# A ViT tower layer on one core: patches of a third image, weight splits, semaphores of biases and running sums, and the order of routing and table steps moved

## Chip, cores, metric

The kernel runs on one core of one Trainium2 chip. The metric is the device time of one execution in microseconds (us). Before the change it was 1286.59 us, the median of three executions (1285.31 to 1288.26).

## What is computed

The reference takes 16 images of 5 x 128 x 128 and computes one tower layer in float32:

- patch embedding: 256 patches of 320 values per image, times W, then a layer norm with gamma;
- attention on the layer-normed tokens, 16 heads of 64: q and k through silu, decay weights exp(cum_i - cum_j) from a running sum of -softplus(x Wa + ba), `attn = (q k) * decay` below the diagonal, `o = attn v`, a norm over each head, a sigmoid gate, the output product, added to the tokens;
- a mixture of experts on the layer-normed result: router logits, softmax, the best 2 of 8 experts, `gelu(x w1 + b1) w2 + b2` of each, weighted and added.

## The kernel before

Each engine has a hand-written stream of instructions, and semaphores tie the streams. The order of the work is the order of the calls in each stream; nothing plans it.

**Start.** SyncE (SP) loads the patches of images 0 and 1, waits for the embedding weight and for image 1's patches, issues the loads of attention weights 0 and 1, then the patches of image 2 (into `xt`, image 0's buffer, so only once image 0 is embedded), then weights 2 and 3. TensorE (PE) runs `tokens(0)`, `tokens(1)`, `turn(0)` (transposes), `tokens(2)`, `turn(1)`, `logits(0)`, the first `queries`, `cum(0)` and so on. Between `tokens` and `turn` lie VectorE's (DVE) `embed` and `embed_norm` and a power on GpSimd (POOL). ScalarE (ACT) and DVE split each weight into a rounded high part (`weight_hi`, line 803) and the rest (`weight_lo`, line 1697); products with split operands take three matmuls. `store_cum` writes the running sums to DRAM in six transfers that count on one semaphore, and `load_decay` reads them back, spread over the partitions, into a ring of four slots (`dec_x`).

**Attention.** Images go in pairs, p = 0 to 7. Step (p, c) with c = 0 to 7 handles two heads of pair p; the same step carries the embedding of pair p + 1, and normalisation, output product and routing of pairs before. `last_step` is c = 7. ACT forms the decays (`decay`, line 838), DVE multiplies them onto the scores (`decayed`, line 1720), PE then runs `weighted` (line 1243). Routing of an image is `turn2` (line 1282, transposes), ACT `keep_x2`, PE `route` (line 1290), DVE `keep_logits` and `choose`, then `ranks`. After 5 pairs (EARLY) `first_tables` (lines 1886 to 1901), 15 small steps on DVE that each wait for the one before, computes from the counts which expert and which rows the first blocks take. It stands in step (7, 0) and waits for a table loaded by `first_constants`.

**Experts.** Rows of tokens were scattered by expert into lists in DRAM. Blocks 0 to 3 (256 rows, plain float32, `early1` line 1339 and `early2` line 1352, one call per chunk c of 8 of the hidden width) are interleaved by hand with the end of attention. Then come whole blocks with split operands (`layer1` line 1538, `layer2` line 1550), and at the end 9 mixed rows: a whole block followed by a unit of 128 rows (`one1` line 1563, `one2` line 1574). Per block, SP loads weights, second-layer bias (`load_b2`, line 414), rows (line 417, or 423 for a unit) and first-layer bias (`load_b1`, line 411). SP also writes padding to the lists (line 597), four transfers in each of two blocks. Both biases of a block count on one semaphore `b_in`, for which ACT waits before the first gelu (line 908) of a block. DVE's `keep_y` (line 1971) adds the second bias, `row_tails` (lines 1957 to 1964) reads token number and router weight from the rows, and `hidden_lo` (line 1987) makes the low part of the hidden values. POOL scales the result (line 716) and adds it to the output by an indirect transfer (line 722), whose landing counts on `added`. SP may refill the row buffer only once `row_tails` has read it.

In `mixed_row`, the stream of DVE before the change is:

```python
for c in range(HC):
    hidden_lo(k, c)
    if c >= HC - WQ and not last:
        w_lo("w1", w1_sp[1 - b_par], w1_stage[1 - b_par], k.b + 1, c - (HC - WQ))
    if c == 2:
        keep_y(before, pieces)
    if c == 4:
        row_tails(k, rows_f[0], BS)
```

## Time and profile before

| | before |
|---|---|
| median of three executions | 1286.59 us |
| profiled execution | 1284.18 us |
| its span, first to last instruction | 1282.3 us |
| PE busy | 1243.4 us (97%), 8534 matmuls |
| ACT, DVE, POOL busy | 858.1, 824.9, 426.6 us |
| mean granted clock of PE | 0.993 of full |

The span runs from the first to the last instruction; 1.9 us of the execution lie around it. A share near 100% names the engine to look at, and the stretches in which that engine stands idle are what other work holds it up for. The granted clock is 1.0 at 2.4 GHz and 0.5 at 1.2 GHz. Times within the span are counted from its start.

### The profile page before, as it was taken

The page shows a single profiled execution, that of the slowest core. Times are in us where ns is not written, and L with a number is a line of the kernel's source. Part 1 is how long each engine was busy: PE and PEld are TensorE (multiplying, and loading weights), DVE is VectorE, ACT ScalarE, POOL GpSimd, SP SyncE. Part 2 cuts the span into 40 slices and gives each one's busy share as a digit, 9 for nine tenths or more (in the row PEclk, how much of TensorE's full clock was granted, in tenths as well). Part 3 has the DMA queues.
Part 4 walks back from the last instruction along what each step waited for, and adds up shares of the span by engine and source line. Part 5 has one row for each costly group of instructions (what it writes and reads, how often), then busy time and mean ns, then how long its engine had stood idle before and what let it go on. Part 6 is the DMA issues. An engine that isn't in the chain of part 4 may idle for free. (4 is left out here: it accounts for less than half of the span.)

```text
span 1282.3 us, 27300 instructions
## 1 busy us (share of the span) xinstructions
PE 1243.4 (97%) x8534; PEld 1068.5 (83%) x8534; DVE 824.9 (64%) x2120; ACT 858.1 (67%) x2019; POOL 426.6 (33%) x524
## 2 busy tenths in 40 slices
PE   6999999999999999999999999999999999999996
PEld 5777788788787877877877777889999999999995
DVE  5455565666666667666566566557788888565561
ACT  4767666667658557567567566447788888666672
POOL 2211121242151241141241151354354454433433
PEclk8999999999999999999999999999999999999998
DMA  5532222233233233232232237288988887989883
GB/s 189 168 101 84 92 88 91 85 113 107 81 115 109 78 117 109 69 126 92 78 123 68 94 118 241 91 239 248 259 230 246 220 225 190 276 264 269 253 238 82
DMA packets 125607, 194.46 MB, mean 152 GB/s; under 512 B 16272, under 2 KB 91504, under 8 KB 125360
## 3 DMA queue, kind: packets, MB, share of 16 engines
q1 hardware_dynamic: 110864, 175.37, 43.1%
q0 software_dynamic: 13584, 17.26, 6.6%
q8 instruction: 54, 0.88, 0.3%
q10 hardware_dynamic: 1056, 0.55, 0.2%
q14 instruction: 49, 0.40, 0.1%
HBM read 167.40 MB, written 29.05 MB: 153 GB/s over the span
## 5 line engine op out<-in xcount | busy, mean ns | idle before, releaser
L1193 PE MATMUL bank<-xn_sp,big_r 128*128 128x512 f32 x1152 | 312.0, 408 | 1.0 <-DVE xn_sp L1692 1.0
L1193 PEld LDWEIGHTS bank<-xn_sp,big_r 128*128 128x128 f32 x1152 | 204.4, 188 | 54.2 <-issue 1.7
L1720 DVE TENSOR_TENSOR att<-bank,dec_x 128x384 f32<-128x384 f32 x256 | 130.5, 551 | 100.6 <-PE bank L1232 95.2
L838 ACT ACTIVATE dec_x<-dec_x,ncum 128x256 f32<-128x256 f32 (+1 forms) x512 | 189.8, 445 | 6.7 <-POOL dec_x L665 6.7
L665 POOL TENSOR_SCALAR_AFFINE_SELECT dec_x<-dec_x 128x256 f32<-128x256 f32 x256 | 108.1, 450 | 226.7 <-DMA dec_x<-cum_scratch 226.2
L1538 PE MATMUL bank<-big_r 128*128 128x256 f32 x1296 | 169.1, 287 | 2.2 <-ACT mid_f L908 2.2
L1538 PEld LDWEIGHTS bank<-big_r 128*128 128x128 f32 x1296 | 162.0, 193 | 3.3 <-ACT mid_f L908 2.4
L716 POOL TENSOR_SCALAR mid_f<-mid_f,dec_x 128x256 f32<-128x256 f32 x71 | 76.3, 1080 | 185.1 <-DVE mid_f L1971 180.0
L1987 DVE TENSOR_TENSOR big_r<-mid_f,big_r 128x256 fp32r<-128x256 f32 x216 | 91.3, 423 | 70.8 <-ACT big_r L928 70.8
L722 POOL DMA_INDIRECT out<-mid_f,tok x71 | 118.8, 1673 | 51.9 <-POOL mid_f L716 21.0
L908 ACT ACTIVATE mid_f<-bank,h 128x256 f32<-128x256 f32 x216 | 101.3, 478 | 42.3 <-PE bank L1538 20.2
L808 ACT ACTIVATE tq<-bank 128x512 f32<-128x512 f32 x64 | 38.3, 598 | 112.9 <-PE bank L1193 112.8
L1978 DVE TENSOR_TENSOR big_r<-big_f,big_r 128x512 fp32r<-128x512 f32 x148 | 101.7, 691 | 8.1 <-ACT big_r L902 1.0
L1186 PE MATMUL bank<-big_r,xn_sp 128*128 128x512 f32 x384 | 98.8, 397 | 0.0
L1271 PEld LDWEIGHTS bank<-big_r,y_sp 128*128 128x128 f32 x768 | 95.5, 191 | 1.9
L1271 PE MATMUL bank<-big_r,y_sp 128*128 128x256 f32 x768 | 96.8, 284 | 0.0
L813 ACT ACTIVATE tq<-bank 128x512 f32<-128x512 f32 x64 | 38.1, 596 | 86.5 <-PE bank L1193 86.4
L902 ACT ACTIVATE big_r<-big_f 128x512 fp32r<-128x512 f32 x148 | 93.6, 637 | 0.0
L928 ACT ACTIVATE big_r<-mid_f 128x256 fp32r<-128x256 f32 x216 | 91.7, 425 | 0.0
L1243 PE MATMUL bank<-att,mid_f 128*64 128x256 f32 x512 | 85.0, 404 | 6.4 <-DVE att L1720 5.0
L687 POOL DMA_INDIRECT expert_rows<-xn,slot x64 | 65.4, 1022 | 76.2 <-DVE slot L1855 60.1
L1229 PE MATMUL bank<-q_s,k_s 64*128 64x256 f32 x512 | 89.9, 428 | 0.3 <-DVE k_s L1711 0.3
(230 smaller groups left out, 2216.2 us busy)
## 6 DMA issues: line engine op xcount, KB each, us to landing
big_f<-in_L_ffn_w SPq DMA_DIRECT2D x68, 1024.0 KB, 7.9
dec_x<-cum_scratch SPq DMA_DIRECT2D x128, 384.0 KB, 3.7
big_w<-in_L_ffn_w SPq DMA_DIRECT2D x12, 1024.0 KB, 6.2
mid_f<-expert_rows SPq DMA_DIRECT2D x27, 261.0 KB, 3.2
h_scratch<-h SPq DMA_DIRECT2D x16, 256.0 KB, 2.3
h<-h_scratch SPq DMA_DIRECT2D x8, 512.0 KB, 4.2
out<-h SPq DMA_DIRECT2D x16, 256.0 KB, 4.1
xt<-in_x SPq DMA_DIRECT2D x15, 256.0 KB, 3.9
```

Source lines behind the costliest of these rows:

```text
L665: pool.affine_select(out=d, in_=d, pattern=[[0, 2], [1, P]], compare_op=ALU.is_ge, fill=fill, base=0, channel_multiplier=-1).then_inc(M["c ...
L722: pool.indirect_dma_start(out=out_rows, out_offset=bass.IndirectOffsetOnAxis(ap=tok[k.par][:, s:s + 1], axis=0), in_=yo[k.par][:, s, :], i ...
L838: act.activation(d, d, ACT.Exp, bias=ncum[p % 2][:, NS * u + s, 2 * c + hh:2 * c + hh + 1]).then_inc(M["exp_done"], 1)
L902: act.activation(parts[0].rearrange("p k n -> p (k n)")[:, cols], staged[:, cols], ACT.Copy).then_inc(M[f"{name}_hi"], 1)
L908: act.activation(target, bank[hbank[c % HB]][:, 0:width], ACT.Gelu_apprx_tanh, bias=b1_sb[k.par][:, c:c + 1]).then_inc(M["gel_done"], 1)
L928: act.activation(g_sp[0][:, c, :], gel[c % NGEL], ACT.Copy).then_inc(M["gh_done"], 1)
L1186: mm = pe.matmul(bank[target][:, :], xp[:, k, t * P:(t + 1) * P], wp[:, k, n * 512:(n + 1) * 512], start=(k == 0 and j == 0), stop=(k == E ...
L1193: mm = pe.matmul(bank[target][:, :], wp[:, k, c * P:(c + 1) * P], xp[:, k, :], start=(k == 0 and j == 0), stop=(k == EC - 1 and j == 2))
L1271: mm = pe.matmul(bank[target][:, s * E:(s + 1) * E], yp[:, j, u * S + s * P:u * S + (s + 1) * P], wp[:, GC * g + j, :], start=(j == 0 and ...
L1538: mm = pe.matmul(bank[hbank[c % HB]][:, 0:BLK], wp[:, i, c * P:(c + 1) * P], xp[:, i, :], start=(i == 0 and j == 0), stop=(i == EC - 1 and ...
L1720: dve.tensor_tensor(att[hh][:, :], bank[4 + hh][:, 0:LW], dec[n % RING][:, hh, :], ALU.mult).then_inc(M["mult_done"], 1)
L1978: dve.tensor_tensor(lo, staged[:, cols], f32(hi), ALU.subtract).then_inc(M[f"{name}_lo"], 1)
```

## The change

- The patches of image 2 get a buffer of their own, slot 3 of the decay ring, and are loaded right after those of image 1; each of the first three images has a semaphore. SP issues the attention weights once the embedding weight and image 0's patches are in.
- PE runs 5 matmuls on zeros before its first wait (`keep_running`), and 5 more between `tokens(1)` and `turn(0)`. A memset of `att0` on DVE feeds them.
- ACT splits weights 1, 2 and 3 later in its stream, behind `keep_xnT(0)`, `xn_hi(0)` and `keep_cum(0)`.
- The running sums of each image of a pair count on a semaphore of their own. So do first-layer and second-layer biases: ACT waits for the first only, `keep_y` for the second.
- `route(11)` moves from step (6, 6) to the last step of pair 6. Around the end of attention, `early1`, `early2`, `gn_mean`, `turn2` and `route` are reordered on PE, and `keep_x2` and the gelus on ACT to fit.
- In the last step of pair 7, DVE runs `decayed(7, 7, 1)` ahead of `head_stats` and `y_lo`.
- `first_tables` moves from step (7, 0) to (7, 2); in its place one copy keeps the counts (`cnt1`).
- In mixed rows `row_tails` follows `keep_y` at c = 2 instead of standing at c = 4.

New semaphore names are left out.

```diff
...
-        side_x = [xt, mid_f[:, 2048:2048 + (KT + 1) * S].rearrange("p (k n) -> p k n", k=KT + 1)]
+        side_x = [xt] + [x.rearrange("p (k n) -> p k n", k=KT + 1) for x in
+                         (mid_f[:, 2048:2048 + (KT + 1) * S], dec_x[:, 3 * 2 * LW:4 * 2 * LW])]
...
+        def patches(n):
+            return side_x[n if n < 3 else 0]
...
         tr1 = room(232, N1)
+        cnt1 = room(242, X)
...
             def load_patches(n):
-                have(sp, "tok_ps", {1: 0, 2: 1}.get(n, n))
-                image, to, m = xT[:, n * S:(n + 1) * S], of(n, side_x), "xt_in1" if n == 1 else "xt_in"
+                have(sp, "tok_ps", n if n > 2 else 0)
+                image, to, m = xT[:, n * S:(n + 1) * S], patches(n), f"xt_in{n}" if n < 3 else "xt_in"
...
                         t = NS * u + s
-                        sp.dma_start(cum_d[p, u, :, cols:cols + P], cumT[t * H:(t + 1) * H, :]).then_inc(M["cum_out"], 16)
+                        sp.dma_start(cum_d[p, u, :, cols:cols + P], cumT[t * H:(t + 1) * H, :]).then_inc(M[f"cum_out{u}"], 16)
...
                 have(sp, "mult_done", 2 * (n - RING + 1))
-                sp.wait_ge(M["cum_out"], 96 * (p + 1))
+                sp.wait_ge(M[f"cum_out{u}"], 48 * (p + 1))
...
             def load_b1(e, par):
-                sp.dma_start(b1_sb[par], b1[bass.ds(e, 1), :, :].rearrange("a p k -> (a p) k")).then_inc(M[f"b_in{par}"], 16)
+                sp.dma_start(b1_sb[par], b1[bass.ds(e, 1), :, :].rearrange("a p k -> (a p) k")).then_inc(M[f"b1_in{par}"], 16)
...
             def load_b2(e, par):
-                sp.dma_start(b2_sb[par], b2[bass.ds(e, 1), :].broadcast_to([P, E])).then_inc(M[f"b_in{par}"], 16)
+                sp.dma_start(b2_sb[par], b2[bass.ds(e, 1), :].broadcast_to([P, E])).then_inc(M[f"b2_in{par}"], 16)
...
             load_patches(1)
+            load_patches(2)
...
             sp.wait_ge(M["wt_in"], 32)
-            sp.wait_ge(M["xt_in1"], 32)
+            sp.wait_ge(M["xt_in0"], 32)
...
             load_weight(1)
-            load_patches(2)
...
                 act.wait_ge(M["ct_ps"], p + 1)
-                have(act, "cum_out", 96 * p)
+                have(act, "cum_out0", 48 * p)
+                have(act, "cum_out1", 48 * p)
...
                 if c == 0:
-                    act.wait_ge(M[f"b_in{k.par}"], 32 * (k.n + 1))
+                    act.wait_ge(M[f"b1_in{k.par}"], 16 * (k.n + 1))
...
             weight_hi(0)
+            keep_xnT(0)
...
             weight_hi(1)
-            keep_xnT(0)
-            weight_hi(2)
...
             xn_hi(0)
-            weight_hi(3)
+            weight_hi(2)
...
             keep_cum(0)
+            weight_hi(3)
...
             keep_x2(2 * NPR - 2)
-            active_early(1, 4)
+            for c in range(4, HC):
+                active_early(1, c)
...
             keep_x2(2 * NPR - 1)
-            for c in range(5, HC):
-                active_early(1, c)
...
         def _(pe):
+            def keep_running(n):
...
+                for i in range(n):
+                    pe.matmul(bank[5][:, 0:E], att[0][:, 0:P], att[0][:, P:P + E], start=True, stop=True)
...
+            pe.wait_ge(M["cleared"], 1)
+            keep_running(5)
...
             pe.wait_ge(M["wt_in"], 32)
-            pe.wait_ge(M["zeroed"], 3)
+            pe.wait_ge(M["zeroed"], 4)
...
             def tokens(n):
-                if n == 1:
-                    pe.wait_ge(M["xt_in1"], 32)
+                if n < 3:
+                    pe.wait_ge(M[f"xt_in{n}"], 32)
...
                 else:
-                    pe.wait_ge(M["xt_in"], 32 * max(n, 1))
+                    pe.wait_ge(M["xt_in"], 32 * (n - 2))
...
                     for k in range(KT + 1):
-                        mm = pe.matmul(bank[embed_bank(n)][:, s * E:(s + 1) * E], of(n, side_x)[:, k, s * P:(s + 1) * P], wt[:, k, :],
+                        mm = pe.matmul(bank[embed_bank(n)][:, s * E:(s + 1) * E], patches(n)[:, k, s * P:(s + 1) * P], wt[:, k, :],
...
                     tokens(2 * p + 4)
+                elif pair(p - 1):
+                    route(2 * p - 1)
...
                     turn2(2 * p - 2, "s1_z", min(p + 2, NPR), 6)
-                if c == 6 and post:
+                if c == 6 and post and p != NPR - 2:
...
             pe.wait_ge(M["c_sum"], 32)
+            keep_running(5)
...
             early1(0, 2)
+            early1(0, 3)
...
             gn_mean(NPR - 1, 1, "lg_done", 2 * NPR - 2)
-            early1(0, 3)
...
             out_proj(NPR - 1, 1, 1, 7, "h2_done", 2 * NPR - 1)
-            early2(0, 4)
-            early2(0, 5)
+            for c in range(4, HC):
+                early2(0, c)
...
             turn2(2 * NPR - 2, "h2_done", 2 * NPR)
-            early2(0, 6)
-            early2(0, 7)
+            early1(1, 4)
+            early1(1, 5)
...
             route(2 * NPR - 2)
-            early1(1, 4)
-            turn2(2 * NPR - 1, "lg_done", 2 * NPR - 1)
-            early1(1, 5)
-            route(2 * NPR - 1)
...
             early1(1, 7)
+            turn2(2 * NPR - 1, "lg_done", 2 * NPR - 1)
...
             early2(1, 0)
+            route(2 * NPR - 1)
...
-            def first_tables():
...
-                dve.wait_ge(M["tb1_in"], 16)
+            def first_counts():
...
                 dve.wait_ge(M["h_out"], 16 * B)
+                dve.tensor_copy(cnt1, cnt).then_inc(M["cnt1_done"], 1)
...
+            def first_tables():
...
+                dve.wait_ge(M["tb1_in"], 16)
+                dve.wait_ge(M["cnt1_done"], 1)
...
                 cmp1 = cut1.rearrange("p (a n) -> p a n", a=N1)
-                t1(dve.tensor_tensor(cut, cnt.rearrange("p (n a) -> p n a", a=1).broadcast_to([P, X, N1]), iob1, ALU.is_ge))
+                t1(dve.tensor_tensor(cut, cnt1.rearrange("p (n a) -> p n a", a=1).broadcast_to([P, X, N1]), iob1, ALU.is_ge))
...
                 dve.wait_ge(M["y_ps"], k.j + 1)
+                dve.wait_ge(M[f"b2_in{k.par}"], 16 * (k.n + 1))
...
                 if main:
+                    if p == NPR - 1:
+                        decayed(p, 7, 1)
...
                     y_lo(p, 0, 0)
-                    decayed(p, 7, 1)
+                    if p < NPR - 1:
+                        decayed(p, 7, 1)
...
                     if p == NPR - 1:
-                        first_tables()
+                        first_counts()
...
                         embed(2 * p + 3)
+                    if p == NPR - 1:
+                        first_tables()
...
+            dve.memset(att[0][:, :], 0.0).then_inc(M["cleared"], 1)
...
                         keep_y(before, pieces)
-                    if c == 4:
...
             def earlier(k):
-                return k._replace(j=k.j - 1, par=1 - k.par, r1=k.r1 - 2)
+                return k._replace(j=k.j - 1, par=1 - k.par, n=k.n - 1, r1=k.r1 - 2)
```

## Rows read from the trace of the kernel before

**Rows 1.** The page, section 1: busy time, share of the span, instructions

```profile
PE 1243.4 (97%) x8534; PEld 1068.5 (83%) x8534; DVE 824.9 (64%) x2120; ACT 858.1 (67%) x2019; POOL 426.6 (33%) x524
```

**Rows 2.** Waits of PE, whole span: total us, times, longest us

```profile
PE bank L1143 <- DMA wt<-in_L_tok_W: 6.2, 1, 6.2
PE bank L1243 <- DVE att L1720: 5.0, 5, 1.7
PE bank L1310 <- DMA mid_f<-expert_rows: 4.3, 5, 1.5
PE bank L1538 <- ACT mid_f L908: 2.2, 1, 2.2
```

**Rows 3.** Windows: length, then busy us (count) PE, PEld, DVE, ACT, POOL; clock, DMA share, GB/s

```profile
25.50:32.30 6.80, 6.42 (x19) 4.56 (x18) 5.45 (x7) 4.31 (x7) 0.00 (x0) 0.50 0.01 2
902.70:906.10 3.40, 3.40 (x18) 3.40 (x18) 2.99 (x6) 3.40 (x10) 0.00 (x0) 0.50 0.88 316
```

**Rows 4.** Timeline of the start, PE and DVE: start us, us, instruction [idle before <-releaser]

```profile
6.23 5.49 PE L1143 MATMUL bank<-wt,xt 128*128 128x256 f32 x12 [6.23 <-DMA wt<-in_L_tok_W]
...
11.51 2.92 PE L1143 MATMUL bank<-wt,mid_f 128*128 128x256 f32 x12
...
11.83 0.70 DVE L1641 BATCH_NORM_STATS2 st<-bank 128x6 f32<-128x512 f32 x1 [10.06 <-PE bank L1143]
```

**Rows 5.** DMA issues of ACT's queue at the start: KB, us to landing (issued at 3.69)

```profile
wa_sb<-in_L_attn_Wa ACTq DMA_DIRECT2D x1, 16.0 KB, 5.4
```

**Rows 6.** Timeline, pair 6 to 7, ACT and the PE instruction that waits

```profile
698.50 0.58 ACT L843 ACTIVATE big_f<-bank 128x512 f32<-128x512 f32 x1
...
699.13 0.65 PE L1243 MATMUL bank<-att,mid_f 128*64 128x256 f32 x4 [1.31 <-ACT big_f L843]
```

**Rows 7.** Timeline, step (7, 0): first and last step of the tables, and PE

```profile
728.03 0.24 DVE L1886 TENSOR_TENSOR h<-taken,xt 128x80 f32<-128x80 f32 x1 [2.76 <-DMA xt<-in_c_first]
...
731.50 0.17 DVE L1901 TENSOR_TENSOR h<-h 128x8 f32<-128x8 f32 x1
...
732.78 0.81 PE L1243 MATMUL bank<-att,mid_f 128*64 128x256 f32 x3 [1.69 <-DVE att L1720]
```

**Rows 8.** Timeline of DVE, end of step (7, 2)

```profile
747.54 1.22 DVE L1762 SCALAR_TENSOR_TENSOR big_f<-big_f 128x1024 f32<-128x1024 f32 x1
750.18 1.02 DVE L1720 TENSOR_TENSOR att<-bank,dec_x 128x384 f32<-128x384 f32 x2 [1.42 <-PE bank L1232]
```

**Rows 9.** Timeline of PE in the same stretch, and at the end of step (7, 7)

```profile
752.96 0.65 PE L1243 MATMUL bank<-att,mid_f 128*64 128x256 f32 x4
...
796.19 0.80 PE L1243 MATMUL bank<-att,mid_f 128*64 128x256 f32 x3 [0.74 <-DVE att L1720]
```

**Rows 10.** Timeline of PE, routing of the last pair

```profile
823.90 1.89 PE L1352 MATMUL bank<-big_w,k_s 128*128 128x256 f32 x8
826.73 0.63 PE L1282 MATMUL bank<-ident,xn 128*128 128x128 f32 x4 [0.94 <-DVE xn L1794]
...
832.04 0.66 PE L1282 MATMUL bank<-ident,xn 128*128 128x128 f32 x4 [1.20 <-DVE lg L1799]
```

**Rows 11.** Timeline, a whole block's first gelu, the rows of PE ahead of and behind it

```profile
896.97 3.04 PE L1550 MATMUL bank<-y_sp,big_r 128*128 128x256 f32 x24
901.65 0.84 ACT L908 ACTIVATE mid_f<-bank,h 128x256 f32<-128x256 f32 x2 [5.32 <-DMA h<-in_L_ffn_b]
```

**Rows 12.** DMA issues from 890.5 to 891.0: KB, us to landing

```profile
big_f<-in_L_ffn_w SPq DMA_DIRECT2D x2, 1024.0 KB, 10.6
```

**Rows 13.** Timeline, first mixed row: DVE, POOL, PE, SP

```profile
1095.50 0.69 DVE L1971 TENSOR_TENSOR mid_f<-bank,tq 128x512 f32<-128x512 f32 x1 [0.36 <-PE bank L1550]
...
1098.32 3.12 PE L1550 MATMUL bank<-big_r 128*128 128x256 f32 x24
...
1100.15 1.60 POOL L722 DMA_INDIRECT out<-mid_f,tok  x1 [1.84 <-DMA out<-mid_f,tok]
...
1102.01 0.37 SPq L417 DMA_DIRECT2D mid_f<-expert_rows  x1
```

More of the change, by code:

```diff
@@ L291, in vit_layer @@
         names = """
-        passed mh_done zeroed c_in c_sum ws_in0 ws_in1 ws_in2 ws_in3 ws_hi ws_lo wt_in g_in
-        xt_in xt_in1 tok_ps s1_st s1_u s1_v0 s1_v1 s1_st2 s1_ve s1_rs s1_h s1_xn
+        cleared passed mh_done zeroed c_in c_sum ws_in0 ws_in1 ws_in2 ws_in3 ws_hi ws_lo wt_in g_in
+        xt_in0 xt_in1 xt_in2 xt_in tok_ps s1_st s1_u s1_v0 s1_v1 s1_st2 s1_ve s1_rs s1_h s1_xn
         s1_tps s1_xnT s1_aps s1_z h_out sp_abs sp_e sp_l sp_m sp_la gnh
-        xh_done xl_done cum_ps cc_done ncum_done ct_ps ct_copied cum_out
+        xh_done xl_done cum_ps cc_done ncum_done ct_ps ct_copied cum_out0 cum_out1
         dec_in0 dec_in1 dec_in2 dec_in3 causal exp_done
@@ L300, in vit_layer @@
         tope_done trec_done wall_done idxf_done pick_done both_done rk_ps rank_done taken_done rsel_done
-        slot_done tail_done scat0 scat1 scat2 scat3 late_out tb1_in tb_in wf_in0 wf_in1 wf_in2 wf_in3 w1_inx tb1
+        slot_done tail_done scat0 scat1 scat2 scat3 late_out tb1_in cnt1_done tb_in wf_in0 wf_in1 wf_in2 wf_in3 w1_inx tb1
         tb pad_out
-        row_in0 row_in1 w1_in0 w1_in1 w2_in0 w2_in1 b_in0 b_in1 xe_ps xe_hi xe_lo w1_hi w1_lo w2_hi w2_lo
+        row_in0 row_in1 w1_in0 w1_in1 w2_in0 w2_in1 b1_in0 b1_in1 b2_in0 b2_in1 xe_ps xe_hi xe_lo w1_hi w1_lo w2_hi w2_lo
         hid_ps gel_done gh_done gl_done y_half y_ps y_done ecol_done wk_done wsel_done y_w added
@@ L1877, in along @@
                 return x.rearrange("p (a n) -> p a n", a=1).broadcast_to([P, n, X])
+            def first_counts():
+                dve.wait_ge(M["taken_done"], EARLY)
+                dve.wait_ge(M["h_out"], 16 * B)
+                dve.tensor_copy(cnt1, cnt).then_inc(M["cnt1_done"], 1)
             def first_tables():
                 dve.wait_ge(M["tb1_in"], 16)
-                dve.wait_ge(M["taken_done"], EARLY)
-                dve.wait_ge(M["h_out"], 16 * B)
+                dve.wait_ge(M["cnt1_done"], 1)
                 cut = cut1.rearrange("p (n a) -> p n a", a=N1)
                 cmp1 = cut1.rearrange("p (a n) -> p a n", a=N1)
-                t1(dve.tensor_tensor(cut, cnt.rearrange("p (n a) -> p n a", a=1).broadcast_to([P, X, N1]), iob1, ALU.is_ge))
+                t1(dve.tensor_tensor(cut, cnt1.rearrange("p (n a) -> p n a", a=1).broadcast_to([P, X, N1]), iob1, ALU.is_ge))
                 t1(dve.tensor_reduce(nb1, cut, AX.X, ALU.add))
```

## The prediction, made before the changed kernel was run

> **What bounds the kernel.** I read the page's busy shares first. PE is busy for 1243.4 us of a span of 1282.3 [rows 1], so everything hangs on PE: its work, its clock, and the 39 us in which it stands idle. The other engines have a third of their time free. The change adds no useful matmul and removes none, so the gain can only come out of idle time and of stretches at the lower clock. The waits of PE [rows 2] are therefore the second view: they tell how much each kind of releaser costs. A busy ScalarE or VectorE elsewhere costs nothing. The third view is the granted clock in windows: 25.5 to 32.3 and 902.7 to 906.1 ran at 0.50, which is 1.2 GHz [rows 3]. PE was idle for 2.17 us just before the second of them [rows 2]. The first 12 matmul records took 5.49 us, the next 12 of the same shape 2.92 us [rows 4], so the start was at the lower level too, although it is not marked as such. Only then do I go to the timeline around each edit. The sum below is made against the profiled execution (1284.18 us, 1282.3 of it span); the median, 1286.59, lies 2.4 us above it, and I subtract the same gain from both.
>
> **1. The start.** Five matmuls on zeros begin after one memset, near 1.3 us. At the cold duration (two records of 5.49 / 12 = 0.46 us each) they take 4.6 us and end near 5.9, before the weight lands at 6.23, so they delay nothing. If they raise the clock, `tokens(0)` takes 2.9 us instead of 5.5 and ends 2.6 us earlier, near 9.1. `embed(0)` follows at 11.83 now [rows 4]. It also waits for the constants on ACT's queue, the last of which was issued at 3.69 and took 5.4 us, so 9.1 [rows 5]. Now image 2's patches (320 KB) and the first attention weights are in flight beside them. I allow 0.5 us for that: `embed(0)` starts near 9.7, 2.1 us earlier than before. Behind it lies a serial chain (DVE, POOL, DVE, PE, twice), then the high parts on ACT, all of which move along; the second five matmuls fill a gap that is otherwise idle. The low parts of the weights were never the last to come while their order on DVE is unchanged, and weights now load about 2 us earlier, so the chain keeps its lead down to the first scores. **2.1 us**, between 0 (clock not raised) and 2.6. The stretch at 0.50 from 25.5 held 6.42 us of busy PE [rows 3], so its removal would give another 3.2; the idle gaps and light matmuls ahead of it stay, so I count nothing and keep 3.2 for the range. Splitting the running sums' semaphore gives nothing: the decays that it releases sooner next queue on ACT behind the same evacuations. If that cover went, it would be worth half a microsecond.
>
> What ACT's queue suffers from a full SP queue is not shown directly. The Trainium skill (DMA: Bandwidth & Descriptors, Queues, rings and completion order) says that every DMA engine takes turns, packet by packet, between the queues that have work, which speaks against loading a third image so early. By that rule the constants share the engines with up to 320 KB more; at some 300 GB/s that would be an estimated 1.1 us instead of my 0.5, and the sum would be 0.6 us smaller.
>
> **2. `route(11)` moved.** PE waits 1.31 us at 699.13 for ACT's copy of 698.50 [rows 6]. The moved matmuls fill that wait and leave the step before shorter. But ACT's copy stands behind a run of ACT work that does not wait for PE, so PE arrives earlier and still starts at 699.13. **0**, between 0 and 1.3. The logits come a little later on DVE; they are read early in the next step, far from the end.
>
> **3. `first_tables`.** In step (7, 0) DVE stands for 2.76 us on a table's load, then works from 728.03 to 731.67, and PE waits 1.69 us for the product behind it [rows 7]. In step (7, 2) the table has landed. DVE is free from 747.54 + 1.22 = 748.8, 3.6 us of tables end at 752.4, and the next product, at 750.18 now [rows 8], starts then. PE wants it at 752.96 [rows 9] and gets its first half some 0.6 us after the start: 0.1 to 0.2 us late. The copy of the counts is one short instruction. The experts' first loads wait for the tables two steps later than before, but stand in step (7, 4) anyway. **1.5 us**, between 1.0 and 1.7.
>
> **4. `decayed(7, 7, 1)` first.** It releases the 0.74 us at 796.19 [rows 9]; `head_stats` and `y_lo` move behind it, and their reader, `gn_mean`, gets one more `early1` ahead of it as cover. **0.7 us**, between 0.3 and 0.7.
>
> **5. Routing of the last pair.** PE waits 0.94 us for the normed rows and 1.20 us for logits [rows 10]. A chunk of `early2` takes 1.89 / 2 = 0.94 us. Four of them from 823.90 on last to 827.6, past 826.73, so the first wait goes. Three more chunks of `early1` stand ahead of the second `turn2`, which is reached near 832.3, past 832.04. Late next are the ranks, since the last `route` now comes after `turn_early(2)` and one chunk while only two chunks cover DVE's choice of experts: 0.25 us. **1.9 us**, between 0.8 and 2.1.
>
> **6. Biases.** At 901.65 ACT had waited 5.32 us for a second-layer bias that the gelu does not read [rows 11]. PE ran dry at 900.0 and lost 2.17 us [rows 2], and then had 3.4 us at half clock [rows 3], worth 1.7. With its own semaphore the gelu starts as soon as ACT is free, near 896.3. `keep_y` waits for the bias instead, most of a row later, when it has landed; `hidden_lo` is queued behind it. What could be late next is the following block's weights: two loads just ahead of that bias took up to 10.6 us [rows 12]. If the first of them landed only then, near 900.8, ACT would stop in its third operation and PE would still lose about 1 us. I take **3.9 us**, since 1 MB ahead of 2 MB should land well before the median of both, between 0.5 and 3.9.
>
> **7. Row tails.** In mixed rows PE waits 5 times for rows of the next whole block, 4.3 us in all, at most 1.5 [rows 2]. SP issues that load right behind the row tails, at 1102.01 in the first mixed row [rows 13]. `keep_y` there starts at 1095.50. Moved behind it, the row tails come up to 3 us earlier, and SP's issue with them. Against it stands a new wait: row tails need the earlier adds to have landed, shown by POOL at 1100.15 [rows 13]. So in this row DVE holds `hidden_lo(3)` until 1100.15 + 1.0 for the tails + 0.4 = 1101.5. PE's second layer, from 1098.32 in four chunks of 0.75, wants it at 1100.6: 0.9 to 1 us lost, and 0.5 of the 1.5 gained here. In the other rows I expect the adds in time. 4.3 - 1.0 = **3.3 us**, between -2 and 4.3.
>
> **Sum.** 2.1 + 0 + 1.5 + 0.7 + 1.9 + 3.9 + 3.3 = 13.4 us. The profiled execution would take 1270.8 us, the median 1286.6 - 13.4 = 1273.2. A measurement of this kernel can tell about 0.2%, or 2.6 us, from no change.
>
> **Rivals.**
> - *The cold stretch at 25.5 goes too.* The work ahead of it shifts by 2 us and has ten more matmuls. For: PE's activity before it changes. Against: the light matmuls and gaps just before 25.5 remain. 13.4 + 3.2 gives 1270.0. Chance 0.17.
> - *Gaps are handed on.* The clock is not raised in time, so that the start gives nothing, and the weights replace the bias at 896 (0.5 instead of 3.9). For: the transfers of [rows 12]. 13.4 - 2.1 - 3.4 = 7.9 gives 1278.7. Chance 0.17.
> - *Slower, through the row tails.* DVE, in nine mixed rows, holds `hidden_lo(3)` behind a landing. PE wants it 5.1 us after `keep_y` starts, and tails and low part take 1.4 of it, so that adds may land 3.7 us after that start; in [rows 13] they land 4.65 after. Each later microsecond costs nine. Without term 7 the gain is 10.1; with a loss of 1.4 us in each row (landings at 5.1 in all nine) it becomes a loss of 2.5, the point from which this decides; at 5.7 it is 18 - 10.1, or 1294.5. Against: PE's waits of today would then shrink too, and `keep_y` waits for almost the same adds already. Chance 0.05.
> - *Nothing to measure.* Every gap comes back behind the next releaser: within 2.6 us of 1286.6. Chance 0.03.
>
> The forecast itself keeps 0.58. The range goes from the first rival with all of term 7 (1269.0, and 1.0 for the scatter of the runs: 1268.0) to the second with term 7 halved (1278.7 + 1.7, about 1280.5). Faster by over 0.2%: 0.58 + 0.17 + 0.17 = 0.92; same 0.03; slower 0.05.
>
> **What would show it.** Term 1: the first `tokens` matmuls near 0.24 us a record, `embed(0)` before 10, the first scores some 2 us earlier. Term 2: PE's wait at the last step of pair 6 longer than 1.31 or ending at the same relative time. Term 3: no wait of DVE for the table, PE's wait in step (7, 1) gone. Terms 4 and 5: those PE waits gone, one of 0.25 before the ranks. Term 6: ACT's wait for a bias absent, clock 1.00 near 900. Term 7: PE's waits for rows at most one. The forecast is wrong if PE idles over 30 us in the new trace, or if new waits of PE for `hidden_lo` fill the mixed rows.

## The result, and the profile after

| | before | after |
|---|---|---|
| median of seven executions | 1286.59 us | 1279.52 us (1274.47 to 1282.02) |
| profiled execution, its span | 1284.18, 1282.3 us | 1277.72, 1275.6 us |
| PE busy | 1243.4 us | 1247.3 us |

The ratio is 0.9933, 95% interval 0.9913 to 0.9953. The ratio goes by all executions and not by the medians: by the medians the changed kernel is 7.1 us faster, by the ratio 8.6, with an interval of 6.0 to 11.2. That is inside the predicted range, but little more than half of the 13.4 us I forecast. (In one of the kernels below, the start undone, one of eight executions took 3056.25 us and counts in no ratio.) The profiled executions differ by as much (6.5 us), so their two traces can be laid side by side, term by term. The page's first line after, which answers to [rows 1]:

```profile
PE 1247.3 (98%) x8554; PEld 1071.8 (84%) x8554; DVE 828.7 (65%) x2123; ACT 857.0 (67%) x2019; POOL 429.5 (34%) x524
```

And of the waits of PE five lines, which answer to [rows 2] (total us, times, longest us):

```profile
PE bank L1322 <- DMA mid_f<-expert_rows: 4.8, 6, 1.7
PE bank L1255 <- DVE att L1733: 2.8, 4, 1.6
PE bank L1155 <- DMA wt<-in_L_tok_W: 1.7, 1, 1.7
PE bank L1563 <- DVE big_r L2006: 0.6, 1, 0.6
PE bank L1311 <- DVE both L1839: 0.4, 1, 0.4
```

The wait for the gelu (2.2 in [rows 2]) and the two for routing [rows 10] are gone, and the waits for attention fell from 5.0 to 2.8. The waits for expert rows, which term 7 was to remove, grew from 4.3 to 4.8 and are now the first line (L1322, before L1310), and a new one for the low part of the hidden values stands behind (L2006). PE's busy time rose by 4 us with twenty records more, those of the matmuls on zeros, which are busy for 6.8 us: busy is not useful here.

**The start.** Timeline of PE and DVE, after (line 1155 was 1143, 1654 was 1641, 1241 was 1229):

```profile
7.43 2.86 PE L1155 MATMUL bank<-wt,xt 128*128 128x256 f32 x12 [1.70 <-DMA wt<-in_L_tok_W]
...
10.88 0.70 DVE L1654 BATCH_NORM_STATS2 st<-bank 128x6 f32<-128x512 f32 x1 [8.31 <-DMA wa_sb<-in_L_attn_Wa]
...
38.92 0.70 PE L1241 MATMUL bank<-q_s,k_s 64*128 64x256 f32 x4 [0.25 <-DVE k_s L1724]
```

The window at the low clock, columns as in [rows 3], and the constant's issue, columns as in [rows 5]:

```profile
22.34:32.60 10.26, 10.13 (x32) 7.89 (x32) 7.22 (x9) 7.66 (x11) 0.00 (x0) 0.51 0.01 2
```

```profile
wa_sb<-in_L_attn_Wa ACTq DMA_DIRECT2D x1, 16.0 KB, 7.2
```

The zeros did what they were to do: the first twelve token matmuls take 2.86 us instead of the 5.49 of [rows 4]. But `embed(0)` waits for the last constant now, which takes 7.2 us instead of the 5.4 of [rows 5], and starts at 10.88 rather than 9.7. And the stretch at 0.50, 6.8 us in [rows 3], lasts 10.3. PE's first scores start at 38.92; before it was 39.02.

**Tables, `decayed` and routing.** PE, after (line 1255 was 1243):

```profile
699.04 0.65 PE L1255 MATMUL bank<-att,mid_f 128*64 128x256 f32 x4 [1.11 <-ACT big_f L849]
...
750.95 0.80 PE L1255 MATMUL bank<-att,mid_f 128*64 128x256 f32 x3 [0.22 <-DVE att L1733]
...
834.75 0.38 PE L1311 MATMUL bank<-both,strict 128*128 128x32 f32 x2 [0.38 <-DVE both L1839]
```

The wait of 1.31 [rows 6] is 1.11 at the same place, and it ends 660.1 us behind the first scores in both kernels, so that moving `route(11)` gave nothing. The 1.69 of [rows 7] is 0.22 two steps later, which makes 1.47. The 0.74 of [rows 9] is gone. Of the 2.14 of [rows 10] there is 0.38 left, before the ranks, where I had put 0.25.

**Biases.** Window 890 to 910, after, same columns:

```profile
890.00:910.00 20.00, 20.00 (x169) 19.91 (x168) 17.22 (x40) 17.54 (x45) 8.51 (x6) 1.00 1.03 307
```

PE is busy throughout at full clock: the 2.17 us and the half-clock stretch of [rows 3, 11] are gone.

**Mixed rows.** Timeline of the first two, after: SP, then DVE, then PE (SP lines 412, 419, 422 load second-layer weights, second-layer bias and rows; DVE 1975 is the first instruction of `row_tails`):

```profile
1089.49 3.42 SPq L419 DMA_DIRECT2D tq<-in_L_ffn_b  x1
1094.28 0.37 SPq L422 DMA_DIRECT2D mid_f<-expert_rows  x1
...
1109.20 1.52 SPq L412 DMA_DIRECT2D big_f<-in_L_ffn_w  x2
1113.41 0.37 SPq L422 DMA_DIRECT2D mid_f<-expert_rows  x1
...
1091.71 0.15 DVE L1975 COPY dec_x<-h 128x1 f32<-128x1 f32 x1 [3.92 <-DMA out<-mid_f,tok]
...
1092.91 0.98 PE L1563 MATMUL bank<-big_r 128*128 128x256 f32 x6 [0.61 <-DVE big_r L2006]
...
1100.29 0.66 PE L1322 MATMUL bank<-ident,mid_f 128*128 128x128 f32 x4 [1.74 <-DMA mid_f<-expert_rows]
...
1120.71 0.66 PE L1322 MATMUL bank<-ident,mid_f 128*128 128x128 f32 x4 [1.03 <-DMA mid_f<-expert_rows]
```

DVE now stands 3.92 us for an add before it can make the low parts, and PE is held up by that. The rows' load in the second row is issued 4.2 us after the pair of weight loads (1109.20 to 1113.41), where before it was 6.2 (SP, then the PE instruction that waits):

```profile
1116.47 1.52 SPq L407 DMA_DIRECT2D big_f<-in_L_ffn_w  x2
...
1122.70 0.37 SPq L417 DMA_DIRECT2D mid_f<-expert_rows  x1
...
1127.67 0.66 PE L1310 MATMUL bank<-ident,mid_f 128*128 128x128 f32 x4 [0.72 <-DMA mid_f<-expert_rows]
```

How long these two loads took, after and before:

```profile
mid_f<-expert_rows SPq DMA_DIRECT2D x1, 261.0 KB, 7.3
mid_f<-expert_rows SPq DMA_DIRECT2D x1, 261.0 KB, 4.9
```

PE, which waits for the landing in both kernels, starts on the rows 11.5 us after the weights' issue now (1120.71) and 11.2 us after it before (1127.67). Over the eight such loads of the mixed rows the issue stands on average 4.7 us behind that of the weights now and 6.2 before, and the landing 11.1 and 10.8. The earlier issue bought nothing. That is the theory the runs had to test: **the rows land behind the 2 MB of weights that SP issued just ahead of them, whenever they are issued.**

### The profile page after: what moved, and what is told of

Same layout as the page of the kernel before. It is cut to its first block and busy times, and to the rows that moved or that the text cites. A ratio compares the mean times of both kernels' runs of the same rounds, so it can differ in the third digit from the quotient of the medians.

```text
span 1275.6 us, 27357 instructions
## 1 busy us (share of the span) xinstructions
PE 1247.3 (98%) x8554; PEld 1071.8 (84%) x8554; DVE 828.7 (65%) x2123; ACT 857.0 (67%) x2019; POOL 429.5 (34%) x524
## 5 line engine op out<-in xcount | busy, mean ns | idle before, releaser
L670 POOL TENSOR_SCALAR_AFFINE_SELECT dec_x<-dec_x 128x256 f32<-128x256 f32 x256 | 111.0, 462 | 213.4 <-DMA dec_x<-cum_scratch 213.1
L2006 DVE TENSOR_TENSOR big_r<-mid_f,big_r 128x256 fp32r<-128x256 f32 x216 | 91.2, 423 | 44.2 <-ACT big_r L934 44.2
```

Source lines behind the costliest of these rows:

```text
L670: pool.affine_select(out=d, in_=d, pattern=[[0, 2], [1, P]], compare_op=ALU.is_ge, fill=fill, base=0, channel_multiplier=-1).then_inc(M["c ...
```

## Experiments

All edits are on the changed kernel, but for the two with the bias alone. Each ratio is to runs of the kernel before beside it. PE's first scores, the mean clock of 12 to 36 us, the first product of the last `ranks` (line 1311), and the time from there to the end of the span split each profiled execution in three parts:

| kernel | median | ratio to before | scores | clock | ranks | ranks to end |
|---|---|---|---|---|---|---|
| before | 1286.59 | | 39.02 | 0.86 | 839.14 | 443.2 |
| bias alone | 1283.94 | 0.9987 [0.9968, 1.0005] | 36.85 | 0.93 | 837.64 | 439.6 |
| bias alone, again | 1284.21 | 0.9975 [0.9960, 0.9989] | 37.70 | 0.93 | 838.12 | 444.5 |
| start undone | 1280.58 | 0.9943 [0.9919, 0.9967] | 37.55 | 0.86 | 833.52 | 445.0 |
| changed | 1279.52 | 0.9933 [0.9913, 0.9953] | 38.92 | 0.79 | 834.75 | 440.9 |
| changed, again | 1277.53 | 0.9930 [0.9910, 0.9949] | 35.81 | 0.93 | 832.67 | 440.8 |
| tails back | 1278.39 | 0.9937 [0.9922, 0.9951] | 37.88 | 0.79 | 834.87 | 439.8 |
| no zeros | 1278.40 | 0.9945 [0.9926, 0.9963] | 38.66 | 0.86 | 834.56 | 441.5 |
| third image late, no zeros | 1280.43 | 0.9939 [0.9919, 0.9960] | 39.93 | 0.79 | 835.78 | 442.9 |
| third image late | 1275.84 | 0.9918 [0.9896, 0.9940] | 34.41 | 1.00 | 830.28 | 443.4 |
| the same, gamma apart | 1274.46 | 0.9910 [0.9888, 0.9932] | 34.66 | 1.00 | 830.51 | 441.3 |
| rows first | 1273.18 | 0.9904 [0.9890, 0.9918] | 37.55 | 0.86 | 833.51 | 437.7 |
| rows first, tails back | 1274.43 | 0.9907 [0.9893, 0.9922] | 37.90 | 0.86 | 835.51 | 439.0 |
| both repairs | 1269.79 | 0.9872 [0.9851, 0.9893] | 34.47 | 1.00 | 830.31 | 435.4 |

Scores to ranks is 795.8 to 796.0 us in eight of the eleven executions with the new middle, 796.9 to 797.6 in the other three, and 800.1 to 800.8 in the three with the old one. The three (the changed kernel again, and both kernels with the tails back) are those in which a stretch at half clock follows PE's wait of 1.11 us near 697. Ranks to end scatters more: in the seven executions with the tails at c = 2 and the rows behind the weights it is 440.8 to 445.0, with the rows ahead 435.4, 437.7 and 439.0.

### Row tails back at c = 4

```diff
                     if c == 2:
                         keep_y(before, pieces)
+                    if c == 4:
                         row_tails(k, rows_f[0], BS)
```

> The changed kernel with row_tails at c == 4 of the mixed row again. Theory Q (the rows wait for the queue: their load lands behind the 2 MB of second-layer weights issued ahead of it on SP's queue, so that moving row_tails earlier gains nothing and only puts the wait for the output adds ahead of the low parts on VectorE): about 1.2 us faster than the changed kernel, PE's waits for rows back near 4.3 us, no wait of PE for big_r in the first mixed row. Theory R (row_tails sets when the rows come, as I forecast, and the profiled executions differ by scatter): 3.3 us slower than the changed kernel, PE's waits for rows higher by that.

1278.39 us, between the two medians of the changed kernel (1279.52 and 1277.53): no difference that can be told. R's loss of 3.3 us is not there; Q's gain of 1.2 us is too small to be told. The waits are as Q had them: 4.6 us for rows, and none for the low part. From its waits of PE:

```profile
PE bank L1322 <- DMA mid_f<-expert_rows: 4.6, 5, 1.7
```

The eight loads of rows are issued 6.2 us behind the weights again, instead of 4.7, and land 10.8 us behind them, instead of 11.1.

### Rows ahead of the second megabyte of weights

```diff
                 load_one(one)
+                bias2(one)
+                rows_only(nxt)
                 weights2_ahead(nxt)
-                bias2(one)
-                rows_whole(nxt)
+                bias1_only(nxt)
```

`rows_only` and `bias1_only` are the two halves of `rows_whole`, each with its own waits; their definitions are left out.

> The changed kernel, in which SP issues the next whole block's rows ahead of that block's second 1 MB of second-layer weights (only one 1 MB load is then ahead of them) and the first-layer bias behind. Theory Q: the rows land some 4 to 5 us after their issue instead of behind two loads, PE's waits for rows fall from 4.8 us to under 1, and the kernel gains 3 to 4 us; the delayed weights must not be late in their turn. Theory R: no gain, or a loss through the weights, and waits for rows as they are.

> Both edits: rows ahead of the second-layer weights, and row_tails at c == 4. Theory Q: with the queue free, the place of row_tails matters again: the rows are issued up to 2 us later than in the kernel with rows first alone. If that still lands in time it is the best of the four, 4 to 5 us below the changed kernel; if not, the waits for rows return in part. Theory R: slower than the changed kernel by 3.3 us.

1273.18 and 1274.43 us. The second differs from the kernel with the tails back by this edit alone and is 4.0 us below it on the same chip; the first is 4.3 below the lower of the changed kernel's medians, and by the ratios to before the gain is 3.3 to 3.9. Waits of PE with rows first:

```profile
PE bank L1565 <- DVE big_r L2016: 1.5, 1, 1.5
PE bank L1336 <- DMA mid_f<-expert_rows: 1.4, 1, 1.4
```

The second mixed row on SP's queue, and how long its rows took:

```profile
1109.11 0.38 SPq L412 DMA_DIRECT2D big_f<-in_L_ffn_w  x1
1110.25 0.33 SPq L419 DMA_DIRECT2D tq<-in_L_ffn_b  x1
1113.02 0.38 SPq L422 DMA_DIRECT2D mid_f<-expert_rows  x1
1114.15 0.38 SPq L412 DMA_DIRECT2D big_f<-in_L_ffn_w  x1
```

```profile
mid_f<-expert_rows SPq DMA_DIRECT2D x1, 261.0 KB, 5.3
```

The rows are issued at the same distance behind the unit's weights as in the changed kernel (3.9 us, there 4.2), but with 1 MB ahead instead of 2 and take 5.3 us instead of 7.3; over all eight it is 3.2 to 5.5 us instead of 5.9 to 7.3. PE no longer waits for them in any mixed row (the 1.4 us are before those). Theory Q holds. (The edit moves two bias loads too. In the first mixed row of the changed kernel SP took 3.42 us to issue one of them behind the 2 MB, here 0.33; what share of the gain is due to that was not tested.) With the tails back as well, the whole span holds only 0.7 us of waits for rows, so with the queue cleared the place of the tails is free; the two kernels do not differ by more than their scatter. What is late next in both is the add, in the first mixed row. With the tails back, from the timeline of DVE and PE, and the window behind:

```profile
1103.67 0.15 DVE L1989 COPY dec_x<-h 128x1 f32<-128x1 f32 x1 [3.66 <-DMA out<-mid_f,tok]
...
1105.18 4.64 PE L1565 MATMUL bank<-big_r 128*128 128x256 f32 x24 [1.95 <-DVE big_r L2016]
```

```profile
1105.50:1108.70 3.20, 3.20 (x18) 3.20 (x17) 2.28 (x4) 2.71 (x8) 2.11 (x2) 0.51 0.89 226
```

PE waited 1.95 us and then ran at half clock, so 24 matmuls took 4.64 us instead of the 3.1 they take elsewhere. These two take back most of the 3.9 us of waits for rows in this one execution, so that its ranks to end is only 0.8 us below that of the tails back (439.0 and 439.8); the other five executions of the kernel have no profile.

### The start: four kernels and the old one

```diff
                 load_patches(1)
-                load_patches(2)
...
                 load_weight(1)
+                load_patches(2)
```

> The changed kernel, in which the third image's patches keep their own buffer but are issued behind attention weights 0 and 1 (as before the change). Theory S (the 320 KB beside the embedding weight and the constants delay both): the weight lands near 6.2 instead of 7.4 us, embed(0) starts near 10 instead of 10.9, PE's first scores come 0.9 us sooner than in an execution of the changed kernel with as long a stretch at half clock. Theory C (the clock sets the rest: how long the stretch at half clock behind 22 us lasts, 6.8 or 10.2 us, decides when the first scores come): embed(0) earlier or not, the scores lie between 37.5 and 38.9 and the whole is the same within 0.5 us.

1275.84 us, 1.7 and 3.7 below the changed kernel's two medians. Timeline of the start with the third image late:

```profile
6.47 2.86 PE L1155 MATMUL bank<-wt,xt 128*128 128x256 f32 x12 [1.37 <-DMA wt<-in_L_tok_W]
...
15.87 2.86 PE L1155 MATMUL bank<-wt,dec_x 128*128 128x256 f32 x12 [1.07 <-DMA dec_x<-in_x]
...
34.41 0.70 PE L1241 MATMUL bank<-q_s,k_s 64*128 64x256 f32 x4 [0.25 <-DVE k_s L1724]
...
9.44 0.70 DVE L1654 BATCH_NORM_STATS2 st<-bank 128x6 f32<-128x512 f32 x1 [6.87 <-PE bank L1155]
```

The constant's issue, and the window of 12 to 36 us:

```profile
wa_sb<-in_L_attn_Wa ACTq DMA_DIRECT2D x1, 16.0 KB, 5.5
```

```profile
12.00:36.00 24.00, 20.31 (x104) 16.00 (x103) 16.64 (x26) 17.98 (x24) 2.84 (x4) 1.00 0.49 168
```

The constant takes 5.5 us again (over all profiles it is 6.5 to 7.7 us in the six with the third image early and 5.1 to 5.7 in the eight others), and `embed(0)` starts at 9.44, released by PE and no longer by a transfer, as theory S said. (The weight is another matter: `tokens(0)`, which waits for it, starts at 6.47 here, and at 7.43 and 5.97 in the two executions of the changed kernel, so its lateness in the first was no effect of the third image that these can show.) Now `tokens(2)` waits 1.07 us for the third image, and that costs nothing. But both theories missed the larger part: there was no stretch at 0.50 at all, so the scores came at 34.41, outside the bounds of theory C.

The second kernel adds a semaphore for gamma:

```diff
-                act.dma_start(dst, src).then_inc(M["c_in"], 16)
+                act.dma_start(dst, src).then_inc(M["gam_in" if dst is gamB else "c_in"], 16)
...
-            dve.wait_ge(M["c_in"], 64)
+            dve.wait_ge(M["gam_in"], 16)
             embed(0)
```

The other waits for `c_in` (PE's ahead of `turn(0)`, and a new one of DVE ahead of `decay_logits(0)`) are for 48 and left out.

> The same edit, and gamma counts on a semaphore of its own, so that embed(0) waits for gamma alone and not for the three constants issued behind it; decay_logits waits for those. Theory S: embed(0) starts as soon as tokens(0) is through, near 9.3 us, and PE's first scores come up to 1.6 us sooner than with all constants in one semaphore. Theory C: the stretch at half clock moves with it and eats most of it, gain under 0.5 us.

1274.46 us. `embed(0)` at 9.24 and scores at 34.66: it waits for PE in either kernel, so gamma's own semaphore gives nothing that can be told. Theory S's first number held. Its 1.6 us did not come against the kernel above, which has all constants on one semaphore (scores at 34.41); against the changed kernel the scores are 1.2 to 4.3 us sooner. Theory C had the gain small, but through a stretch at half clock that is not there. The medians differ by 1.4 us, less than either interval can tell.

Next the matmuls on zeros are left out, which no part of the result hangs on: both `keep_running(5)` calls are deleted, with the third image early as changed, then late.

> The changed kernel without its ten matmuls on zeros (no part of the result hangs on them). Theory S (the early start is limited by the transfers of the weight, the constants and the third image, and the raised clock only hides in that): the first 12 token matmuls take 5.5 us again and the second 12 end near 15.8, embed(0) starts near 13, and PE's first scores come about 2 us later than at 38.9 if that chain sets them; the kernel is 1 to 2.5 us slower. Theory U (the ten matmuls raise nothing that lasts, the longer stretch at half clock behind takes it back): no difference within 0.5 us.

> Third image late, and no matmuls on zeros (no part of the result hangs on them). Theory K (the late third image alone keeps the clock up behind 22 us): no stretch at 0.50 there, first scores near 37. Theory M (the matmuls on zeros are needed for that too: they bring the chain forward and fill the gap ahead of turn(0)): 6.8 us at 0.50 behind 25 us as before the change, first scores near 38.5 to 39, and the kernel 2 to 4 us slower than with late patches and the matmuls.

1278.40 and 1280.43 us. Without the zeros the token matmuls are slow again (5.46 us for the first twelve in both), the scores come at 38.66 and 39.93, and the mean clock of 12 to 36 is 0.86 and 0.79. With the third image early, the medians do not tell the zeros from no zeros, as theory U had it; of S's steps only the slow matmuls came, since `embed(0)` starts at 11.46 and not near 13, and the scores are no later than in the changed kernel's first execution. With it late the zeros are worth 4.6 us by the medians and 2.7 by the ratios, whose intervals overlap, and 5.5 us in the scores of the profiles. That is theory M, with a stretch at half clock of some 10 us where it had 6.8. Theory K fails. **In the profiles neither edit alone gains; the two together do.**

Then all of the start is undone (buffer, semaphores, SP's order, zeros, and the splits of weights 1 to 3 in their old places):

> The changed kernel with its start as before the change: third image into the first image's buffer, no matmuls on zeros, weights split in the old order, the semaphore order of SP as before. It keeps the biases, tables, routing and row tails, and the split semaphore of the running sums. Theory S: the start of the change is worth about 1.1 us (first scores at 37.9 in the middle of four executions of the same start, against 39.0 before), so this is 1 us slower than the changed kernel. Theory N (start worth nothing): the same. By my forecast it would be 2.1 us slower.

1280.58 us, and the scores at 37.55. Four executions with the old start have them at 36.85, 37.55, 37.70 and 39.02, five with the changed start at 35.81, 37.55, 37.88, 37.90 and 38.92: means of 37.8 and 37.6. By these rows the start as changed is worth 0.2 us, but they scatter over 2 to 3 us, and the whole kernel does not settle it: this one is 1.1 and 3.1 us above the changed kernel's two medians, and 1.3 and 1.7 by the ratios. That is nearer to theory S than to N, and neither they nor my forecast of 2.1 can be excluded. What the rows do show is how little of the shift of `embed(0)` was left: it starts at 10.7 to 11.8 in the four and at 10.4 to 11.4 in the five, 0.6 us earlier in the mean and not 2.1. In the three kernels with zeros and a late third image the scores are at 34.41 to 34.66.

### The biases alone, on the kernel before

```diff
-                    act.wait_ge(M[f"b_in{k.par}"], 32 * (k.n + 1))
+                    act.wait_ge(M[f"b1_in{k.par}"], 16 * (k.n + 1))
...
                 dve.wait_ge(M["y_ps"], k.j + 1)
+                dve.wait_ge(M[f"b2_in{k.par}"], 16 * (k.n + 1))
```

> The kernel before, with nothing changed but the two semaphores of first-layer and second-layer biases. Theory B (PE's wait of 2.17 us and the 3.4 us at half clock behind it both hang on the bias that the gelu does not read): 3.9 us faster than before, and no stretch at 0.50 near 903. Theory W (the weights are late there next): PE waits about 1 us in the same place, and the gain is 1 to 3 us.

> The kernel before with the split bias semaphores once more: its profiled execution had gained 5.1 us, the middle of its 12 executions 2.7 us. Theory B (3.9 us, in every execution): the middle near 1282.7. Theory P (only part: PE's wait of 2.2 us always goes, the 3.4 us at half clock behind it came in some executions of before alone, or comes elsewhere): the middle between 1283.5 and 1284.5.

1283.94 and 1284.21 us, 2.7 and 2.5 below the medians of before beside them (1286.65 and 1286.72). The ratios give 1.7 and 3.2, and their intervals reach from a loss of 0.6 to a gain of 4.1 us and from 1.4 to 5.1, so they do not exclude 3.9. In both profiles PE is busy and at full clock from 890 to 910, as theory B said, and the wait of [rows 11] is gone. The second then has two stretches at 0.50 later, each behind a wait for rows (a third wait, of 1.73 us at 1188.29, has none behind it, and neither has one of 1.88 in the first). Timeline of PE and the windows of that kernel:

```profile
1102.75 1.04 PE L1310 MATMUL bank<-ident,mid_f 128*128 128x128 f32 x4 [1.87 <-DMA mid_f<-expert_rows]
...
1146.28 0.66 PE L1310 MATMUL bank<-ident,mid_f 128*128 128x128 f32 x4 [2.19 <-DMA mid_f<-expert_rows]
```

```profile
1102.80:1106.10 3.30, 3.30 (x16) 3.30 (x17) 1.83 (x8) 2.12 (x6) 2.45 (x2) 0.51 0.46 164
1147.20:1150.50 3.30, 3.30 (x16) 3.21 (x15) 2.56 (x5) 3.29 (x9) 2.46 (x2) 0.51 0.41 69
```

The two medians and these rows speak for theory P: the 2.2 us went both times, and the 1.7 us of the clock can be lost again in other places. Which share is lost stays open.

### The changed kernel again, and both repairs

> The changed kernel itself once more, beside the others on one chip. If its 1279.5 us is its typical time, 1278 to 1280 again; its first scores then come between 37.5 and 38.9 us, depending on how long the half clock behind 22 us lasts. If its first profiled start was a poor draw, 1277 to 1278.

> The changed kernel with both repairs: third image behind attention weights 0 and 1, gamma on a semaphore of its own, and the whole block's rows ahead of its second-layer weights. If the two act apart, their gains add: 4 us from the start (first scores at 34.7 instead of 38.9, when no stretch at half clock comes) and 3 to 4 us from the rows, so near 1270 us, 7 below the changed kernel. If the clock merely falls elsewhere (the wait for adds in the first mixed row was followed by half clock in one execution), 1272 to 1274.

1277.53 and 1269.79 us. The changed kernel's profile has its scores at 35.81, a better draw than any of the other four, and then a half-clock stretch at a wait that the first profile also has (699.04, above) without one. PE and the window of that execution:

```profile
695.99 1.12 PE L1255 MATMUL bank<-att,mid_f 128*64 128x256 f32 x4 [1.11 <-ACT big_f L849]
```

```profile
696.00:699.30 3.30, 3.30 (x17) 2.19 (x18) 2.63 (x4) 2.77 (x3) 0.00 (x0) 0.50 0.72 220
```

With both repairs the kernel is 7.7 us below the changed one on the same chip. Alone, on other chips, they gave 3.1 us (1274.46 against 1277.53) and 4.3, so the gains add. 1269.8 is the 1270 that was expected of it. Its page, one of PE's waits, and its scores:

```profile
PE 1240.9 (98%) x8554; PEld 1069.0 (84%) x8554; DVE 828.4 (65%) x2123; ACT 857.1 (68%) x2019; POOL 430.1 (34%) x524
```

```profile
PE bank L1566 <- DVE big_r L2017: 1.0, 1, 1.0
```

```profile
34.47 0.70 PE L1256 MATMUL bank<-q_s,k_s 64*128 64x256 f32 x4 [0.25 <-DVE k_s L1739]
```

No wait for expert rows is on its list any more, and PE is busy 6.4 us less than in the changed kernel's first profile for the same 8554 matmuls, at a mean granted clock of 0.997 against 0.993: most of that is clock. (This was the fastest of its five executions.)

## Why the prediction was half right

The sum was 2.1 + 0 + 1.5 + 0.7 + 1.9 + 3.9 + 3.3. The first pair of profiles gives, in the same order, 0.1, 0, 1.5, 0.7, 1.8, 3.9 and -1.2, which is 6.8 for a difference in span of 6.7. (The -1.2: waits for rows 4.3 to 4.8, the new wait 0.6, and 0.1 for the rest.) The tails back gave no difference that can be told, so term 7 is about nothing and not a sure loss. The total fell inside the range because the five other terms carried it: 13.4 without terms 1 and 7 is 8.0.

- **Terms 2 to 5 were right** as a sum: from scores to ranks the eleven executions with the new middle take 4.2 us less in the mean than the three with the old one (4.1 to 5.0 in the eight without the half clock near 697), against 4.1 forecast. None of the four was taken back by itself, so the share of each is read from PE's waits alone. The terms rested on rows of DVE and PE with their times, and on what was queued behind each.
- **Term 1 failed in its size: `embed(0)` "starts near 9.7", and the chain behind it, "all of which move along".** Two things took the 2.1 us. The last constant took 1.8 us longer than in [rows 5], not 0.5, so that `embed(0)` started at 10.88. The Trainium skill (DMA: Bandwidth & Descriptors, Queues, rings and completion order) has the engines take turns between queues packet by packet, which I had turned into an estimated 1.1 us. The traces agree with its direction: the same 16 KB take 7.0 us in the mean of six profiles with the third image early and 5.4 in the eight others. And I counted the stretch at 0.50 as fixed, with 3.2 us on the upside alone. Its length added up to between nothing and 10.3 us in these executions, about half of which is lost time, and with the chain's start moved it could as well grow. With the third image late and the zeros `embed(0)` did start at 8.7 to 9.4, and the scores came 3.3 us before the mean of the old start.
- **Term 7 failed in its mechanism: "Moved behind it, the row tails come up to 3 us earlier, and SP's issue with them."** SP's issue came earlier relative to the weights, by 1.5 us in the mean of eight loads and 2 us in the second row (in the first it came later, 7.1 us behind them against 6.4, behind that bias of 3.42 us). But I took the landing to follow the issue. It followed the 2 MB ahead in the same queue, and the load's durations tell as much: 3.2 us in the median of its 27 issues, and 5.9 to 7.3 us in the eight mixed rows. With that the 3.3 us that the term was to bring are missing. The new wait of DVE for the adds, which I charged to the first row alone, stood in most rows, mostly unnoticed by PE; in the first row the adds landed 4.6 us behind the start of `keep_y`, as I had it, and PE lost 0.6 us where I had 0.9 to 1.
- **Term 6 was right in the profile**, and perhaps too large for the median, where 2.5 to 2.7 us of it show: the 1.7 us of clock can be lost again behind other waits.

The rival in which the start gives nothing was the nearer one for term 1, but its other half (weights late at 896) did not happen, and it kept term 7 whole. That its 1278.7 lies within 1 us of the measured 1279.52 is luck: two errors of 3.4 and 3.3 us cancel. My sign of being wrong, PE idle over 30 us, did not come (28.3), but only because the matmuls on zeros count as busy; without their 6.8 us it is 35, less than before by 4.

## What to carry to other kernels

When a load is late, look at what was issued ahead of it on its queue, and in what size, before moving the instruction that releases it; a small load that is wanted soon goes ahead of a large one that is wanted late. Two edits of a serial start, a prefetch and a warm engine, can each be worth nothing alone and 3 us together, or spoil one another, so try each with and without the other. And price a wait of PE with what the clock may add behind it, over several executions: in the 14 profiles half clock followed 3 of the 52 waits of 1.0 to 1.8 us, 3 of the 7 of 1.87 to 2.02 us and all 5 of 2.08 to 2.75 us (counted behind the first 36 us).

## What was not expected of the hardware

- The same program has stretches at half clock in different places from one execution to the next: behind the same wait of 1.11 us near 697, one execution of the changed kernel stayed at 1.00 and the other ran 3.3 us at 0.50. Of the eleven executions with that wait three did, and their scores to ranks is 1.0, 1.1 and 1.7 us longer than in the others. Between 12 and 36 us they add up to nothing, or to about 3.4, 6.8 or 10.2 us (the mean clocks of the table, taken over 24 us).
- In all three executions with the matmuls on zeros and the late third image the clock stayed at 1.00 from 12 to 36 us; in the eleven others its mean was 0.79 to 0.93. What about PE's work decides it stays open: busy time in 12 to 22 us was 7.2 to 8.1 us in the three, and 7.5 in the changed kernel's first execution, which had the longest stretch. Nor is it shown that every execution of those kernels is so: each has one profile, and two of the three profiled were the fastest of their kernel.
